# Bucket transfers behind the edge loop, and one indirect transfer underway behind it

## The reference

```python
edge_index = jnp.stack([src, dst])
x = x + _L0_gnn_ref(_layernorm(x), edge_index, ...)   # per edge: a score of 8 heads from both ends, softmax over all nodes
x = x + _L0_ffn_ref(_layernorm(x)[None], ...)[0]      # 6 experts
x = x + _L1_gnn_ref(_layernorm(x), edge_index, node_vec1, ...)  # 4 blocks: sparse attention over the edges, then an MLP
x = x + _L1_ffn_ref(_layernorm(x)[None], ...)[0]      # 16 experts, top-2 routing with a capacity
x = x + _L2_gnn_ref(_layernorm(x), edge_index, edge_type_8, edge_weight, ...)  # messages from h[src] summed at dst
x = x + _L2_ffn_ref(...)[0]
x = x + _L3_gnn_ref(...)
x = x + _L3_ffn_ref(...)[0]
```

## Time and profile before

| | us |
|---|---|
| median of 3 runs | 1986.03 |
| lowest, highest | 1964.48, 2000.69 |
| span of the profiled execution | 1997.1 |

### The profile page before, as it was taken

One profiled execution on the slowest core, in us unless ns is written; L12 is line 12 of the kernel. 1 busy time (PEld: TensorE's weight loads), 2 busy tenths in 40 slices (PEclk: granted clock), 3 DMA queues, 4 the chain that ended last, 5 costly groups with the idle time before them and its releaser, 6 DMA issues.

```text
span 1997.1 us, 22478 instructions
## 1 busy us (share of the span) xinstructions
PE 1645.9 (82%) x6977; PEld 889.3 (45%) x7007; DVE 901.9 (45%) x2072; ACT 501.2 (25%) x1607; POOL 609.0 (30%) x656
## 2 busy tenths in 40 slices
PE   5988786889879897999599596257779999999888
PEld 3533333334455453646255374143234455555455
DVE  8865565558764433343225315296662210111322
ACT  1122232234653231413113121141020011111233
POOL 6744453443204265454610251505710000000000
PEclk9988898889879897999699798678889999999999
DMA  7210010010242312233021671607622512211020
GB/s 281 73 26 17 17 49 13 16 49 18 75 92 64 115 46 79 71 74 76 24 70 63 143 274 56 179 1 186 185 84 64 194 64 89 69 63 48 5 64 17
DMA packets 122492, 159.45 MB, mean 80 GB/s; under 512 B 51945, under 2 KB 64505, under 8 KB 122034
## 3 DMA queue, kind: packets, MB, share of 16 engines
q1 hardware_dynamic: 92448, 113.04, 18.2%
q0 software_dynamic: 22112, 30.02, 5.8%
q10 hardware_dynamic: 7858, 15.44, 2.4%
HBM read 142.52 MB, written 15.94 MB: 79 GB/s over the span
## 4 chain that ended last, share of the span: by engine, by line
PE 66%; DVE 15%; another core or an unknown queue 10%; issue 6%; ACT 2%; DMA 1%; POOL 0%; DVEq 0%; ACTq 0%; POOLq 0%
PE psum L379 64%; DVE arena L2570 2%; DVE stats L470 1%; DVE ring L656 1%; DVE mask_dst L1351 1%; DVE ring L1337 1%; DVE xn L2009 1%; DVE ring L1273 1%; DVE xn L2015 1%; PE psum L1007 1%; DVE arena L1340 0%; DVE xn L2028 0%; PE psum L1839 0%; PE psum L2229 0%
## 5 line engine op out<-in xcount | busy, mean ns | idle before, releaser
L379 PE MATMUL psum<-arena 128*128 128x24 bf16 (+8 forms) x2026 | 329.9, 317 | 80.7 <-issue 42.6
L379 PE MATMUL psum<-arena,ring 128*128 (+1 forms) x1478 | 365.8, 389 | 23.0 <-issue 19.3
L379 PE MATMUL psum<-xT,ring 128*128 128x384 f32 x928 | 319.8, 506 | 10.8 <-ACT ring L3004 4.2
L379 PE MATMUL psum<-ring,arena 128*128 128x512 f32 (+1 forms) x592 | 277.6, 617 | 24.6 <-DVE ring L656 18.9
L379 PEld LDWEIGHTS psum<-arena 128*128 128x128 bf16 (+5 forms) x2026 | 198.0, 147 | 222.0 <-issue 130.1
L379 PE MATMUL psum<-ring,xT 128*128 128x512 f32 x552 | 252.1, 609 | 2.3 <-DMA bc<-in_wide 1.2
L379 PEld LDWEIGHTS psum<-xT,ring 128*128 128x128 f32 x928 | 183.1, 199 | 144.0 <-issue 33.6
L379 PEld LDWEIGHTS psum<-arena,ring 128*128 128x128 bf16 (+1 forms) x1504 | 147.7, 120 | 162.9 <-issue 79.2
L1337 DVE SCALAR_TENSOR_TENSOR ring<-psum,wa 128x1024 f32<-128x1024 f32 x104 | 127.2, 1223 | 158.1 <-remote 101.8
L1058 ACT ACTIVATE ring<-ring 128x128 f32<-128x128 f32 x416 | 123.3, 297 | 286.6 <-DVE ring L1337 240.4
L379 PEld LDWEIGHTS psum<-ring,arena 128*128 128x128 f32 (+1 forms) x592 | 104.9, 192 | 153.9 <-issue 152.8
(11 more groups left out here) (462 smaller groups left out, 1660.3 us busy)
## 6 DMA issues: line engine op xcount, KB each, us to landing
ring<-in_L_ffn_w SPq DMA_DIRECT2D x22, 1024.0 KB, 6.4
ring<-in_L_gnn_m_w SPq DMA_DIRECT2D x8, 1024.0 KB, 6.3
ring<-in_L_ffn_expert_weights SPq DMA_DIRECT2D x8, 1024.0 KB, 6.8
ring<-tab_key ACTq DMA_DIRECT2D x24, 256.0 KB
ring<-in_L_gnn_Wv SPq DMA_DIRECT2D x5, 1024.0 KB, 5.4
tab_w<-xn SPq DMA_DIRECT2D x6, 768.0 KB, 15.0
ring<-in_L_gnn_Ww SPq DMA_DIRECT2D x4, 1024.0 KB, 7.6
ring<-in_L_gnn_wq SPq DMA_DIRECT2D x4, 1024.0 KB, 6.2
```

The costliest lines, as they stand in the source:

```text
L379: return nc.tensor.matmul(o, a, b, start=start, stop=stop)
```

## The change

All 76 bucket transfers of the edge loop move to POOL's code of the L1 graph layer, which follows the loop directly in POOL's queue; they stand there behind a few `iota` instructions and ahead of the store of the bases. `few_underway` takes the number in flight as an argument: 2 (`IN_FRONT`) for the 20 buckets ahead of the loop, 1 (`BEHIND_LOOP`) for all others, for the bases and for the records. The two waits on banks of PE (`f0h10`, `l1k0_3`) among the bases are taken out.

```diff
@@ -285,14 +285,13 @@
         node_base = sem("node_base")
         base_stored = sem("base_stored")
         ranks_landed = sems("ranks_landed", UN)
-        BESIDE_F0 = 34
         BUCKETED, BASES, RECORDS = 0, ET // UN, ET // UN + ST // UN
-        UNDERWAY = 2
-
-        def few_underway(pool, q, earlier):
-
-            if q >= UNDERWAY:
-                k = q - UNDERWAY
+        IN_FRONT, BEHIND_LOOP = 2, 1
+
+        def few_underway(pool, q, earlier, most):
+
+            if q >= most:
+                k = q - most
                 pool.wait_ge(ranks_landed[k % UN], 16 * (earlier + k // UN + 1))
         bucketed_loaded = sem("bucketed_loaded")
         bucketed_cleared = sem("bucketed_cleared")
@@ -838,6 +837,11 @@
         SINGLE = 2 * UN
         AHEAD = 20
 
+        def to_bucket(pool, q, most):
+            few_underway(pool, q, BUCKETED, most)
+            nc.gpsimd.indirect_dma_start(tab_bucketed, bass.IndirectOffsetOnAxis(ap=pos[:, q:q + 1].bitcast(U32), axis=0),
+                                         rec[:, q, :], None).then_inc(ranks_landed[q % UN], 16)
+
         def unit_name(u):
             r, q, t = UNITS[u]
             return f"l0uv{r}{q}{t}"
@@ -1138,15 +1142,10 @@
                     last = nc.gpsimd.tensor_scalar(slot_one[:, g % 2, j, :], iota[:, 0:P], q_f[:, t:t + 1], None, ALU.is_equal)
                 last.then_inc(slot_hot, 1)
 
-            def to_bucket(q):
-                few_underway(pool, q, BUCKETED)
-                nc.gpsimd.indirect_dma_start(tab_bucketed, bass.IndirectOffsetOnAxis(ap=pos[:, q:q + 1].bitcast(U32), axis=0),
-                                             rec[:, q, :], None).then_inc(ranks_landed[q % UN], 16)
-
             pool.wait_ge(bucketed_cleared, 16)
             pool.wait_ge(pos_ready, 1)
             for q in range(AHEAD):
-                to_bucket(q)
+                to_bucket(pool, q, IN_FRONT)
             pool.wait_ge(filled, 96)
             pool.wait_ge(pair_ready, 1)
             for q in range(ST):
@@ -1158,8 +1157,6 @@
                     pool.wait_ge(w_landed, 16 * q)
                 nc.gpsimd.indirect_dma_start(tab_w, bass.IndirectOffsetOnAxis(ap=pair[:, q:q + 1].bitcast(U32), axis=0),
                                              w_edge0[:, q, :], None).then_inc(w_landed, 16)
-                if q + AHEAD < ET:
-                    to_bucket(q + AHEAD)
 
         @on("dve")
         def _(dve, od):
@@ -2085,6 +2082,8 @@
             nc.gpsimd.iota(gate[NF:2 * NF, 7, 0:1], pattern=[[0, 1]], base=1, channel_multiplier=1,
                            allow_small_or_imprecise_dtypes=True).then_inc(consts_ready, 1)
 
+            for q in range(AHEAD, ET):
+                to_bucket(pool, q, BEHIND_LOOP)
             pool.wait_ge(node_base, 1)
             nc.gpsimd.dma_start(tab_base.rearrange("(p q) k -> p (q k)", p=P), base_all).then_inc(base_stored, 16)
 
@@ -2093,11 +2092,8 @@
             nc.gpsimd.dma_start(rec[:], tab_bucketed.rearrange("(q r) k -> r q k", r=P)).then_inc(bucketed_loaded, 16)
             base_got = base_all
             pool.wait_ge(base_stored, 16)
-            banks.filled(pool, "f0h10")
             for q in range(ST):
-                if q == BESIDE_F0:
-                    banks.filled(pool, f"l1k0_{HA - 1}")
-                few_underway(pool, q, BASES)
+                few_underway(pool, q, BASES, BEHIND_LOOP)
                 pool_gather(base_got[:, q:q + 1], tab_base, base_at[:, q:q + 1]).then_inc(ranks_landed[q % UN], 16)
             for b in range(UN):
                 pool.wait_ge(ranks_landed[b], 16 * (BASES + ST // UN))
@@ -2108,7 +2104,7 @@
             pool.wait_ge(bucketed_loaded, 16)
             pool.wait_ge(sorted_cleared, 16)
             for q in range(ST):
-                few_underway(pool, q, RECORDS)
+                few_underway(pool, q, RECORDS, BEHIND_LOOP)
                 nc.gpsimd.indirect_dma_start(tab_sorted, bass.IndirectOffsetOnAxis(ap=pos2[:, q:q + 1].bitcast(U32), axis=0),
                                              rec[:, q, :], None).then_inc(ranks_landed[q % UN], 16)
 
```

## The result

The changed kernel takes 2135.81 us (median of 4 runs, 2118.60 to 2142.14) against 1993.36 us (4 runs, 1964.48 to 2013.13) for the kernel before: ratio 1.080, 95% interval 1.065 to 1.095. It is slower by 142 us at the medians. Some executions of a kernel fall into a slower state, and all ratios in this text leave those out and compare means, so that a ratio is not always the quotient of the medians beside it (here it is 2133.1 against 1975.3). The two profiled executions have spans of 2116.6 and 1997.1 us, 119.5 us apart; the one after is the fastest of its four runs, so this distance is on the small side.

The account below looks back on a forecast made before the run. TensorE carried 66% of the chain, with some 200 us of unknown waits. POOL's string was to become the bound, its shift of +101 us taking the span from 1997.1 to 2098, hence a median of 2088 us; range 1966 to 2180.

Parts of the forecast that it names:

- The forecast: Whole kernel: POOL's string becomes the new bound with the loop's stalls gone, 2088 us, own range 2034 to 2147; chance 0.75.
- (b): POOL's strings behind the loop: 284 single transfers, 3.1 us each until 982, then 2.4 in quiet; through at 1236.
- (c): L1 expert layer's dispatch, queued behind POOL: routing ready at 982, POOL through at 1236, everything behind shifts by +101 us.
- (a): Edge loop: with 76 buckets out, groups take about 11.7 us and stalls go; 108 us gained, POOL leaves at 418.
- 178 transfers until 982: POOL's strings: number done at 3.1 us each from 430 until the routing is ready, leaving 106 at 2.4 us.
- p: POOL's strings: whole time of one transfer, issue to landing; bounds 2.35 and 3.1, mean 2.84, break-even 2.48 us.
- The waits on banks: Base gathers: the two waits on TensorE's banks go and no longer hold anything, as POOL is late anyway.
- Rival 1: POOL's strings: lone transfers not delayed by weight loads; 1948 us at 2.35 each, 1833 at under 1.94; chance 0.12.
- fixed cost of about 2.0 us: POOL's strings: the skill's figure per POOL-issued DMA; as whole price it gives a shift of -137 us.
- Rival 2: Edge loop: stalls don't come from the buckets and stay; shift +221 us, 2207 us; chance 0.08.
- Rival 3: Whole kernel: no effect, POOL's lateness and the gain cancel or both are small; 1966 to 2006 us; chance 0.05.
- a late page: Edge loop: possible stall mechanism, an instruction page fetched late behind dense small transfers; no row showed it, no size given.

Follow-up runs that it names:

- run with 24 buckets: The changed kernel with 72 of its 96 bucket transfers left out, the 24 others issued ahead of the loop: 1973.73 us, ratio 1.006 on the second chip.
- pairs: The changed kernel with the transfers behind the loop issued two at a time, then waiting for a landing: 1943.89 us, ratio 0.971 on the third chip.
- move alone: The changed kernel with two underway everywhere and the bank waits kept: 1786.82 us, ratio 0.997 on the first chip; 1947.43 us on the second.
- 52 buckets: The changed kernel with paired transfers behind the loop and 52 buckets back in it, one behind every second score: 1867.28 us, ratio 0.931, third chip.

## Why the prediction was right, point by point

**The forecast held**: POOL's string is the new bound, and the stalls of the loop are gone. The median is 2135.81 us where 2088 was predicted, inside the range and 48 us above the point. The span is 2116.6 against 2098: 31 us more from the string (b), 13 less from the stretch behind it (c). The other 29 us aren't explained by the sum: it put the median 10 us under the profiled span, as it had been before, and now it lies 19 us above, since the profiled execution is the fastest of the four.

**(a) The loop** was right: groups of 11.7 us (expected 11.7), no wait on "remote" (near zero), last score at 420.27 (418 for its end, it was 421.2). There the gain was real and full. What I left out is that it isn't a property of the kernel: on the first chip there was nothing to gain. That the result was measured where the stalls exist is luck for the size of the forecast. And "the stalls go with the buckets" was right only because the change also thins them; moved but dense, they stall what stands behind the loop.

**(b) The price of a transfer** was slightly too low, the mis-sized term. The model wanted 178 transfers until 982 at 3.1 us; by the spacings it was 3.24 on average, 178 x 0.14 = 25 us. In quiet it was 2.46 against 2.4, some 6 us over 104. The fixed parts, the end of the loop with them, came out within 2 us in sum. Together +31, and the dispatch was at 1267.2 instead of 1236. As a mean over all, p = (1267.2 - 430) / 284 = 2.95, in the forecast's own range of 2.65 to 3.05. That p is two things, as the run with 24 buckets showed: 2.4 us for a transfer, and a delay of some 150 us that belongs to the stretch with weight loads; priced so, the sum would also hold for another number of transfers.

**(c) The queue behind**: a punctual dispatch at 977.2 (predicted 982), as the L1 graph layer lost its stalls too (attention parts of 71.0 to 71.5 us; 87.4 and 100.2 before in blocks 0 and 2); six dispatch scatters right behind the last record; TensorE idle for 305 us, where "some 200" was written, though the prediction's own times give 1236 - 982 = 254. The stretch behind the dispatch was 12.9 us shorter, where I had it unchanged; stalls stand in it in both kernels, and their length differs from run to run (849 to 869 us on these chips).

**The waits on banks** were rightly costed at nothing: the first gather goes at 670.97, when the attention part of block 0 is over (641.19), and the 103 behind it wait for landings alone.

**Rival 1**, transfers alone not delayed, is refuted by 2.44 to 11.73 us within the string of gathers. By the Trainium skill (DMA: Bandwidth & Descriptors, "Anatomy of one DMA - SWDGE (gpsimd) path") a fixed cost of about 2.0 us would have turned the sign. The trace doesn't agree with 2.0 us as the whole price: the row at 1176.58 shows 1.39 us of waiting behind 0.97 us of issue, 2.36 us from start to start in quiet, so a chain of dependent transfers must be priced with the issue in it. **Rival 2**, stalls from elsewhere in the loop, is refuted by the clean loop. **Rival 3**, gain and loss cancel, would have needed p near the break-even of 2.48; measured p is half a microsecond above it.

**What stays open** is why engines stall. Shown is where: on two of three chips (and in the first measurement), beside runs of POOL's transfers at 1.26 us, and not with one underway, in pairs or in threes in those strings (the pairs and threes weren't tried in the L2 graph layer's gathers). In the case looked at in detail TensorE then starts its instructions about 1.4 us apart without waiting for data. Not every long run has a stall beside it, and on the first chip none has. The Trainium skill (Runtime: NRT & Kernel Launch, "Instruction fetch mechanics") has sequencers fetch pages over a queue of their own, and the prediction thought of a late page. The rows speak against it. All that the instruction queues moved in the kernel before from 130 to 450 us, where all 18 stalls of the loop end, and in the move alone on the second chip from 470 to 500 us, where TensorE is late again and again (queue: packets, MB, share of the DMA engines):

```profile
q14 instruction: 1, 0.01, 0.0%
...
q14 instruction: 1, 0.01, 0.1%
```

One packet each, where each of those stalls would need a late one. As far as the profile records these queues in full, late pages don't make these stalls; what does isn't known.

How many transfers in a row it takes wasn't tested on purpose, but the kernel before has shorter runs. Four from 265.46 on stand beside a group without a stall (12.84 us); six from 402.38 on, the last of them below, end with one:

```profile
408.92 0.96 POOL L1143 DMA_INDIRECT tab_bucketed<-rec,pos  x1 [0.30 <-issue]
411.20 1.22 DVE L1337 SCALAR_TENSOR_TENSOR ring<-psum,wa 128x1024 f32<-128x1024 f32 x1 [3.10 <-remote]
```

In the run with 24 buckets, five in a row from 101.94 on and then three go before the 3.17 us at 113.39. These are single cases and give no limit.

On the first chip the changed kernel wasn't run: 1267 + 812 = 2079 us would be 1.16 of before there, an estimate.

## What to carry to other kernels

Before a queue of small transfers is made to wait for each landing, count them and price the string from issue to landing, and ask when the queue must be through: here 284 x 2.4 us plus 150 us of delay put POOL 290 us behind the places that it waited for before, where it had been 127 us ahead. A density that disturbs others can be broken with far less than full serialization: pairs kept the stalls away at 0.74 to 0.85 of the price (buckets 2.36 against 3.20 us, records 2.09 against 2.46). And spread the transfers over the time in which their queue waits anyway, the edge loop here: 52 buckets cost nothing in it, and 81 us until the dispatch behind it even in pairs (1080 against 999).

## What was not expected of the hardware

- The same kernel takes 1790 us on one chip and 1994 to 2009 us on two others, with spreads of 15 and some 50 to 90 us. Most of the difference stands where the stalls are: the four traces of the first chip have none, and in the two traces of the kernel before there are 93 and 102 us in the loop, attention parts longer than 71.5 us by 20 and 46 us in all, and stretches behind the dispatch longer than the first chip's 812 us by 44 and 50.
- The gathers of the L2 graph layer, 31 at 1.25 us, go with stalls of others too, in the changed kernel as well (not on the first chip). POOL's first ones, and DVE in its timeline:

```profile
1389.61 0.95 POOL L625 DMA_INDIRECT arena<-tab_h,sd_t  x1 [0.30 <-issue]
1390.86 0.95 POOL L625 DMA_INDIRECT arena<-tab_h,sd_t  x1 [0.30 <-issue]
...
1401.53 0.26 DVE L2558 TENSOR_REDUCE arena<-psum 128x32 f32<-128x96 f32 x1 [11.60 <-remote]
...
1429.72 0.26 DVE L2558 TENSOR_REDUCE arena<-psum 128x32 f32<-128x96 f32 x1 [26.22 <-remote]
```

  Pairs there are the next thing to try; it wasn't done.
- While PE, DVE and ACT were idle, TensorE's granted clock was 0.50 (its level of 1.2 GHz), yet in the 200 us behind the dispatch it was 0.76 on average, against 0.77 before; the hole cost nothing beyond itself.
